# Gate and up from whole-number weights, with the scales applied where PSUM is read, in a quantized FFN on one core

## The chip, the cores and the metric

One NeuronCore of a Trainium2 chip runs the whole program. The metric is the device time of one launch in microseconds, as a median over runs. A profile is one further execution, recorded by the hardware.

## The reference

For x of 2 x 1024 x 512 in float32, `out = x + s * silu(f)`, where s is causal attention with ALiBi over the layer-normed x (32 heads of 16) and f is a gated FFN with int4-like weights on the same normed x. What matters here is the FFN. The weights are whole numbers 0 to 15, with a zero point and a scale for each group of 128 rows and each column:

```python
def dequantize(imatrix, scales, zeros, group_size, out_dtype):
    rs = jnp.repeat(scales, group_size, axis=0)
    rz = jnp.repeat(zeros, group_size, axis=0)
    return ((imatrix.astype(rs.dtype) - rz.astype(rs.dtype)) * rs).astype(out_dtype)
gate = silu(dot(x, gate_proj)); up = dot(x, up_proj)      # 512 -> 1792
f = dot(gate * up, down_proj)                             # 1792 -> 512
```

The group of 128 rows is just one contraction step k of TensorE (512 = 4 x 128). So within one k the scale depends on the output column alone.

## The kernel before

The program is three stages, one after the other: projections and layer norms (0 to about 190 us of the profile), attention in 16 groups of 4 heads (to about 764 us), and the last stage, which is output projection, FFN and combination (764 us to the end).

**Float32 as two parts.** A float32 operand is split into a rounded `fp32r` high part (ACT, a copy) and the rest (a subtraction, DVE or POOL). A product of two such operands takes three matmuls: low x high, high x low, high x high (`terms`).

**In the attention stage** the FFN's weights are made ready beside the attention. A "half job" is 128 x 896 weights: SP loads zeros (broadcast), scales (broadcast) and weights, ACT converts weights and zeros to float (`convert`), POOL subtracts (L799) and multiplies (L802) in the weight buffer `w_f`. There are 24 of them, 16 for gate and up and 8 for down. POOL also forms small vectors for the softmax in between (`chain`), in program order with the jobs.

**In the last stage** the loop `blocks` runs over 4 blocks of 512 tokens (three in a hardware loop, the last by itself). The 4 quarters (u or t) of a block are 128 tokens each. Each block does:
- the attention output of 4 quarters is gathered (ACT `load_o`), transposed (PE L1279, `trans_o`), split (ACT `hi_o`, DVE L1230 `lo_o`) and projected (PE L1301, 12 matmuls for each quarter) into the four single banks `y`; ACT copies the result to `s_sb` (`copy_s`);
- 14 tiles `it` of 128 inner columns. `gate_up` (L1318) is 2 x 4 x 3 = 24 matmuls of 512 columns into a pair of banks, gate in one and up in the other, each an accumulation over all four k. ACT takes Silu of the gate bank (L1188), DVE multiplies by the up bank (L1251) and that is h; ACT copies its high part (`h_hi`), DVE subtracts for the low part (L1253); `down` (L1330) is 12 matmuls into `y`. The weights of each tile are split too: ACT copies three high parts of 128 x 512 (`w_gu`, `w_d`, L1130) and POOL subtracts three low parts (L1089);
- at the end ACT takes Silu of the four `y` banks (L1214), DVE multiplies by `s_sb` (L1262), POOL or DVE adds x (L1124, L1266), SP stores.
- the normed x of the next block is made in between (DVE L1225 `norm`, PE L1288 `trans_x`, ACT `hi_x`, DVE L1236 `lo_x`).

PE's order for a tile is `gate_up(it + 1)` and then `down(it)`, so the chain from the gate bank to the low part of h has a whole `gate_up` to run behind. The eight PSUM banks are four single ones (`y`) and two pairs (`pair`). All orders are written out by hand, each engine runs its own in program order, and semaphores join them.

Of the kernel before, what the change touches and what calls it, by code (L numbers as in the profile page):

```python
# [24 lines left out]
F32 = mybir.dt.float32  # L25
# [7 lines left out]
P = 128  # L33
# [19 lines left out]
ROWS = 111  # L53


def build(nc, x, wproj, lnw, w_all, z_all, s_all, ident_in, identb_in, tri_in, behind_in, qrows, krows, out):
# [7 lines left out]
    with ExitStack() as ctx:  # L64
# [16 lines left out]
        xrstd = sb("xrstd", [P, TILES], F32)  # L81

# [18 lines left out]
        with ExitStack() as ca:  # L101
# [13 lines left out]
            vst = sa("vst", [P, 2, HEADS, VW], F32)  # L115
            st6x = sa("st6x", [P, 6], F32)
# [8 lines left out]
        w_f = sb("w_f", [P, JOBS * INNER], F32)  # L125
# [16 lines left out]
        with ExitStack() as cc:  # L142
            sc = sb_in(cc)
            xc_hi = sc("xc_hi", [P, KT, 512], F32R)
            xc_lo = sc("xc_lo", [P, KT, 512], F32R)

            ws_hi = [sc(f"ws_hi{n}", [P, 3, 512], F32R) for n in range(2)]
            ws_lo = [sc(f"ws_lo{n}", [P, 3, 512], F32R) for n in range(2)]

            h_hi = [sc(f"h_hi{n}", [P, 512], F32R) for n in range(2)]  # L150
            h_lo = [sc(f"h_lo{n}", [P, 512], F32R) for n in range(2)]
            sg = [sg0, sc("sg1", [P, 512], F32)]
            xnc = sc("xnc", [P, 2, D], F32)
# [132 lines left out]
        cst_in, lnw_in, wo_in = sem("cst_in"), sem("lnw_in"), sem("wo_in")  # L286
        wo_hi_done, wo_lo_done = sem("wo_hi_done"), sem("wo_lo_done")
# [33 lines left out]
        with nc.Block() as block:  # L321
            @block.sync
            def _(sp):
                sp.dma_start(xin[:, 0, :], x_t[0]).then_inc(x_in[0], 16)
                for kt in range(KT):
# [6 lines left out]
                  .then_inc(lnw_in, 16)  # L332

# [88 lines left out]
            def _(act):  # L422
# [50 lines left out]
                def body(c, s, q, first, last):  # L473
                    for u in range(2):
                        t = 2 * c + u
                        copy_v(t, u, c)
                        if not (last and u == 1):
                            x_hi(t + 1, 1 - u)
                        if u == 1 and not first:
# [155 lines left out]
            def _(pe):  # L635
# [24 lines left out]
                def qk_trans(t):  # L660
                    for a in range(2):
                        pe.wait_ge(qk_ln, 2 * t + a + 1)
                        if not (isinstance(t, int) and t < 1):
                            pe.wait_ge(part_r, 2 * t - 1 + a)
                        for kt in range(KT):
# [5 lines left out]
                def body(c, s, q, first, last):  # L671
                    for u in range(2):
                        t = 2 * c + u
                        project(t, u, 2, b_v, proj_v, (v_copy, t))
                        if not (last and u == 1):
                            x_trans(t + 1)
                        project(t, u, 0, b_q, proj_q, (qk_clip, 2 * t - 1))
# [33 lines left out]
        z_in, z_conv, z_sub, z_mul = sem("z_in"), sem("z_conv"), sem("z_sub"), sem("z_mul")  # L711

# [21 lines left out]
        with nc.Block() as block:  # L736
            @block.sync
            def _(sp):
                def half_job(jj):

                    if not (isinstance(jj, int) and jj == 0):
                        sp.wait_ge(z_mul, jj)
                    sp.dma_start(zst[:, :].bitcast(I32), z_all[bass.ds(jj, 1), :].to_broadcast([P, HALF])).then_inc(z_in, 16)
                    sp.dma_start(sst[:, :], s_all[bass.ds(jj, 1), :].to_broadcast([P, HALF])).then_inc(z_in, 16)
                    sp.dma_start(w_f[:, bass.ds(jj * HALF, HALF)].bitcast(I32), w_all[bass.ds(jj, 1)].rearrange("a p c -> (a p) c"))\
# [5 lines left out]
                half_job(0)  # L751
# [680 lines left out]
```

## Time and profile before

| | us |
|---|---|
| median of 3 runs | 1297.69 |
| the 3 runs | 1294.58, 1297.69, 1305.38 |
| span of the profiled execution | 1300.7 |
| PE busy in it | 1205.7 (93%) |
| DVE, ACT, POOL busy | 754.4, 626.0, 503.3 |

The busy time of PE counts matmuls that overlap: a matmul of 512 columns is recorded as 0.39 us and the next one starts 0.23 us after it. So the busy share tells that PE has work, not that it runs at its peak. To see the pace one reads starts. "L1330" is a line of the kernel as printed above. "x12" in a merged row is twelve instructions in a row, and a time in square brackets is the idle time before it with the instruction that ended it.

### The profile page before, as it was taken

To read this page: it belongs to the slowest core of one execution; us is meant where nothing else is said; L and a number is where in the kernel's file an instruction comes from. 1 tells how busy PE (TensorE), PEld (TensorE's weight loads), DVE (VectorE), ACT (ScalarE), POOL (GpSimd) and SP (SyncE) were. 2 spreads that over 40 slices of the span, in tenths; PEclk is the share of its full clock that TensorE was granted. 3 is DMA by queue.
4 is the path that set the end of the run, shared out by engine and by line. 5 is a ranking of instruction groups with operands and counts; after the bars stand their busy time and mean duration, and the time that the engine had idled before them with its cause. 6 is when DMAs were issued, how large, how long until landed. Compare 5 with 4: busy or idle time off the path is not lost. (4 is left out here: it accounts for less than half of the span.)

```text
span 1300.7 us, 23572 instructions
## 1 busy us (share of the span) xinstructions
PE 1205.7 (93%) x6848; PEld 768.9 (59%) x6848; DVE 754.4 (58%) x1835; ACT 626.0 (48%) x955; POOL 503.3 (39%) x544
## 2 busy tenths in 40 slices
PE   6999987999999899899998989999999999999997
PEld 5777752333333333333333358887888888888886
DVE  6877887877877778778777622225222522252223
ACT  3333332666666566566665764335433443344332
POOL 2755550313131221212131333555455445545553
PEclk9999986999999999999999989999999999999999
DMA  6234454454546444555565210001100010011000
GB/s 222 91 115 131 138 163 133 116 144 105 147 105 143 99 118 84 125 107 149 107 149 108 83 69 1 1 1 40 57 0 0 32 65 0 0 33 65 1 1 33
DMA packets 101901, 106.62 MB, mean 82 GB/s; under 512 B 28385, under 2 KB 81121, under 8 KB 101729
## 3 DMA queue, kind: packets, MB, share of 16 engines
q1 hardware_dynamic: 75392, 93.10, 27.7%
q10 hardware_dynamic: 26464, 12.98, 3.4%
q8 instruction: 22, 0.36, 0.1%
q14 instruction: 23, 0.18, 0.0%
HBM read 84.41 MB, written 21.23 MB: 81 GB/s over the span
## 5 line engine op out<-in xcount | busy, mean ns | idle before, releaser
L842 ACT ACTIVATE pr<-pair 128x1024 f32<-128x1024 f32 (+3 forms) x384 | 293.6, 811 | 179.7 <-PE pair L965 101.3
L1089 POOL TENSOR_TENSOR ws_lo<-w_f,ws_hi 128x512 fp32r<-128x512 f32 x168 | 238.0, 1445 | 271.8 <-ACT ws_hi L1130 271.8
L264 DVE CUSTOM_DVE_ANT_0 bank<-bank,sg 128x384 f32<-128x384 f32 (+3 forms) x512 | 242.3, 515 | 97.7 <-PE bank L274 94.4
L1251 DVE TENSOR_TENSOR sg<-pair,sg 128x512 f32<-128x512 f32 x56 | 38.8, 692 | 276.0 <-ACT sg L1188 276.0
L1318 PE MATMUL pair<-xc_hi,ws_lo 128*128 128x512 f32 x448 | 175.4, 392 | 0.0
L1318 PE MATMUL pair<-xc_lo,ws_hi 128*128 128x512 f32 x448 | 175.2, 391 | 0.0
L1318 PE MATMUL pair<-xc_hi,ws_hi 128*128 128x512 f32 x448 | 175.1, 391 | 0.0
L267 DVE TENSOR_REDUCE mx<-bank 128x1 f32<-128x512 f32 x256 | 159.8, 683 | 7.4 <-PE bank L274 6.7
L1188 ACT ACTIVATE sg<-pair 128x512 f32<-128x512 f32 x56 | 33.5, 598 | 235.7 <-PE pair L1318 235.6
L799 POOL TENSOR_TENSOR w_f<-w_f,zst 128x896 f32 (+1 forms) x24 | 50.1, 2088 | 215.2 <-ACT zst L856 215.2
L274 PE MATMUL bank<-xin_c,s_sb 108*128 108x512 bf16 (+3 forms) x384 | 118.3, 354 | 13.1 <-DVE mx L264 10.2
L274 PE MATMUL bank<-ks,qs 108*128 108x512 bf16 (+3 forms) x384 | 111.6, 337 | 7.9 <-DVE mx L264 6.9
L1130 ACT ACTIVATE ws_hi<-w_f 128x512 fp32r<-128x512 f32 x168 | 99.1, 627 | 30.2 <-PE bank L1330 28.4
L960 PE MATMUL pair<-qs,ks 111*128 111x512 bf16 (+3 forms) x384 | 97.1, 338 | 16.2 <-DMA qs<-dt 10.4
L960 PE MATMUL pair<-s_sb,xin_c 111*128 111x512 bf16 (+3 forms) x384 | 97.5, 339 | 14.9 <-DMA s_sb<-dt 10.6
L1253 DVE TENSOR_TENSOR h_lo<-sg,h_hi 128x512 fp32r<-128x512 f32 x56 | 71.1, 1271 | 47.7 <-ACT h_hi L1130 47.7
L1318 PEld LDWEIGHTS pair<-xc_hi,ws_hi 128*128 128x128 f32 x448 | 84.6, 189 | 17.7
L1318 PEld LDWEIGHTS pair<-xc_hi,ws_lo 128*128 128x128 f32 x448 | 84.6, 189 | 17.5
L1318 PEld LDWEIGHTS pair<-xc_lo,ws_hi 128*128 128x128 f32 x448 | 84.4, 188 | 17.5
L274 PEld LDWEIGHTS bank<-xin_c,s_sb 108*128 108x128 bf16 x384 | 34.3, 100 | 93.8 <-DVE mx L264 52.2
L1330 PE MATMUL bank<-ws_hi,h_lo 128*128 128x512 f32 x224 | 88.0, 393 | 0.4 <-DVE h_lo L1253 0.2
L1330 PE MATMUL bank<-ws_hi,h_hi 128*128 128x512 f32 x224 | 87.3, 390 | 0.0
(101 smaller groups left out, 1980.0 us busy)
## 6 DMA issues: line engine op xcount, KB each, us to landing
stk<-parts ACTq DMA_DIRECT2D x16, 768.0 KB, 5.9
zst<-in_z_all SPq DMA_DIRECT2D x24, 448.0 KB, 4.2
sst<-in_s_all SPq DMA_DIRECT2D x24, 448.0 KB, 5.0
w_f<-in_w_all SPq DMA_DIRECT2D x24, 448.0 KB, 6.8
xin_c<-in_x SPq DMA_DIRECT2D x32, 256.0 KB, 2.7
s_sb<-stk SPq DMA_DIRECT2D x96, 64.0 KB
xin_c<-stk SPq DMA_DIRECT2D x96, 64.0 KB
qs<-stk SPq DMA_DIRECT2D x96, 64.0 KB
```

What stands on the lines that cost most here:

```text
L264: dve.tensor_tensor_reduce(out=src, in0=src, in1=tri[:, 512 - w:512], scale=1.0, scalar=-3.0e38, op0=ALU.add, op1=ALU.max, accum_out=dst). ...
L267: dve.tensor_reduce(dst, src, AX.X, ALU.max).then_inc(m_free, 1)
L274: pe.matmul(b[:, 0:w], qs[s][0:ROWS_MAX, qt // 4, j, (qt % 4) * P:(qt % 4 + 1) * P], ks[s][0:ROWS_MAX, j, k0:k0 + w], start=True, stop=Tru ...
L799: pool.tensor_tensor(w, w, zst[:, :], ALU.subtract).then_inc(z_sub, 1)
L842: act.activation(pr[e % 3][:, 2 * p:2 * p + 2, 0:w], pair[p][:, :, 0:w], ACT.Exp, scale=SCALE)\
L960: mm = pe.matmul(pair[p][:, jj, 0:512 - c0], ks[s][0:ROWS, j, kt * P:(kt + 1) * P], qs[s][0:ROWS, qb, j, c0:512], start=True, stop=not dia ...
L1089: return pool.tensor_tensor(dst, src, hi.bitcast(F32), ALU.subtract)
L1130: return act.activation(dst, src, ACT.Copy)
L1251: dve.tensor_tensor(sg[s][:, :], pair[s][:, 1, :], sg[s][:, :], ALU.mult).then_inc(h_mul, 1)
L1253: dve.tensor_tensor(h_lo[s][:, :], sg[s][:, :], h_hi[s][:, :].bitcast(F32), ALU.subtract).then_inc(hl_done, 1)
L1318: mm = pe.matmul(pair[s][:, g, :], l, r, start=(k == 0 and n == 0), stop=(k == KT - 1 and n == 2))
L1330: mm = pe.matmul(y[t][:, :], l, r, start=(it == 0 and n == 0), stop=(it == IT - 1 and n == 2))
```

## The change

All of it concerns the FFN.

1. **Weights.** Gate and up weights stay whole numbers after the zero point is taken off (w - z, from -15 to 15). These fit `fp32r` without a rest. So there are no low and high parts of gate and up weights any more: `w_gu` on ACT and POOL is gone, and matmuls read `w_gu`, now the name of the weight buffer itself. In the attention stage POOL's job for these 16 halves is one subtraction (out of a staging buffer) and not two operations; the scale is not loaded in broadcast. The 8 half jobs of down are as before.
2. **Scales.** A small table `sgu` holds the scales with the inner column on the partition: one DMA, one transpose and one ACT copy in the first stage.
3. **Matmuls.** For each tile and each of gate and up, each k has a bank of its own: 8 banks for a tile, 2 matmuls each (w x low part of x, w x high part of x). That is 16 and not 24. The banks are the four of the two pairs (`GB`), used in turn: bank j needs bank j - 4 to be read.
4. **Reading the banks.** ACT reads the k = 0 banks with a scale (`first`, twice for a tile); DVE reads the other six with `scalar_tensor_tensor`: bank * scale + accumulator (`add`). ACT's Silu then works in SBUF, and so does DVE's multiplication (`gate`, two SBUF operands).
5. **Low parts of h and of the down weights** are both made by POOL, in this order for a tile: `h_low(it)`, `w_low(it)`. DVE makes neither.
6. **Order.** PE does all of `gate_up(it)` and then `down(it - 1)` (for tiles 4 to 13). The projection of the attention output is cut in half quarters and lies between the banks of tiles 0 to 2; it uses `y` banks for its transposes, not the pair. ACT's order for a tile is `silu(it - 1)`, `first(it, 0)`, `first(it, 1)`, `h_high(it - 1)`, `w_high(it - 1)`.

The core of the diff:

```diff
-                def w_gu(b, it):
-                    s = it % 2
-                    pool.wait_ge(wg_hi, IT * b + it + 1)
-                    for n in range(2):
-                        mm = low(ws_lo[s][:, n, :].rearrange("p (k c) -> p k c", k=KT), w_cols(n, it),
-                                 ws_hi[s][:, n, :].rearrange("p (k c) -> p k c", k=KT))
-                    mm.then_inc(wg_lo, 1)
...
+                def h_low(b, it):
+                    pool.wait_ge(hh_done, IT * b + it + 1)
+                    pool.tensor_tensor(h_lo[it % 3][:, :], acc[0][it % 2][:, :], h_hi[it % 3][:, :].bitcast(F32), ALU.subtract)\
+                        .then_inc(hl_done, 1)
+
+                def w_low(b, it):
+                    pool.wait_ge(wd_high, IT * b + it + 1)
+                    pool.tensor_tensor(wd_lo[it % 2][:, :], w_down(it), wd_hi[it % 2][:, :].bitcast(F32), ALU.subtract)\
+                        .then_inc(wd_low, 1)
 
                 def body(b, last):
                     for it in range(IT):
...
+                        h_low(b, it)
+                        w_low(b, it)
...
+                def first(b, it, n):
+
+                    act.wait_ge(hl_done, IT * b + it + 1)
+                    act.wait_ge(gu_done, IT * NJ * b + NJ * it + n + 1)
+                    act.activation(acc[n][it % 2][:, :], GB[n], ACT.Copy, scale=scale_of(n, 0, it)).then_inc(ev_first, 1)
+
+                def silu(b, it):
+                    act.wait_ge(ev_add, (NJ - 2) * (IT * b + it) + NJ - 3)
+                    act.activation(acc[0][it % 2][:, :], acc[0][it % 2][:, :], ACT.Silu).then_inc(silu_done, 1)
+
+                def h_high(b, it):
+                    act.wait_ge(h_mul, IT * b + it + 1)
+
+                    act.wait_ge(down_done, C_D + IT * b + it - 2)
+                    copy(h_hi[it % 3][:, :], acc[0][it % 2][:, :]).then_inc(hh_done, 1)
...
+                    for it in range(IT + 1):
+                        if it > 0:
+                            silu(b, it - 1)
+                        if 1 <= it <= 2:
+                            copy_s(b, 2 * it - 2)
+                        if it < IT:
+                            for n in range(2):
+                                first(b, it, n)
+                        if it < 2:
+                            hi_o(b, 2 * it)
+                            load_o(b, 2 * it + 1)
+                        if it == 0:
+                            hi_o(b, 1)
+                            load_o(b, 2)
+                        else:
+                            h_high(b, it - 1)
+                            if it <= 2:
+                                copy_s(b, 2 * it - 1)
+                            if it == 1:
+                                hi_o(b, 3)
+                            w_high(b, it - 1)
...
+                def add(b, it, j):
+
+                    n, k = j % 2, j // 2
+                    dve.wait_ge(gu_done, IT * NJ * b + NJ * it + j + 1)
...
+                    a = acc[n][it % 2][:, :]
+                    dve.scalar_tensor_tensor(out=a, in0=GB[j % 4], scalar=scale_of(n, k, it), in1=a, op0=ALU.mult, op1=ALU.add)\
+                       .then_inc(ev_add, 1)
...
                 def body(b, last):
                     for it in range(IT):
...
+                        if it > 0:
+                            gate(b, it - 1)
+                        for j in range(2, NJ):
+                            add(b, it, j)
+                            if it < 2 and j in (3, 5):
+                                lo_o(b, 2 * it + (j - 3) // 2)
...
+                def gate_up(b, it, pair_of):
+
+                    for j in (2 * pair_of, 2 * pair_of + 1):
+                        n, k = j % 2, j // 2
+                        if j < 4:
+                            if it > 0:
+                                pe.wait_ge(ev_add, (NJ - 2) * (IT * b + it - 1) + j + 3)
+                            elif j == 0:
+                                pe.wait_ge(xc_l, 4 * b + 4)
+                        elif j < 6:
+                            pe.wait_ge(ev_first, 2 * (IT * b + it) + j - 3)
+                        else:
+                            pe.wait_ge(ev_add, (NJ - 2) * (IT * b + it) + j - 5)
+                        w = w_col(n, k, it)
+                        pe.matmul(GB[j % 4], w, xc_lo[:, k, :], start=True, stop=False)
+                        pe.matmul(GB[j % 4], w, xc_hi[:, k, :], start=False, stop=True).then_inc(gu_done, 1)
+
+                def down(b, it, t):
+                    if t == 0:
+                        pe.wait_ge(wd_low, IT * b + it + 1)
+                        pe.wait_ge(hl_done, C_HL + IT * b + it + 1)
...
+                    gate_up(b, 0, 0)
                     trans_o(b, 0)
-                    gate_up(b, 0)
+                    gate_up(b, 0, 1)
                     trans_o(b, 1)
+                    gate_up(b, 0, 2)
+                    s_project(b, 0, 0)
+                    gate_up(b, 0, 3)
+                    s_project(b, 0, 1)
+
+                    gate_up(b, 1, 0)
                     trans_o(b, 2)
+                    s_project(b, 1, 0)
+                    gate_up(b, 1, 1)
+                    s_project(b, 1, 1)
+                    gate_up(b, 1, 2)
                     trans_o(b, 3)
+                    s_project(b, 2, 0)
+                    gate_up(b, 1, 3)
+                    s_project(b, 2, 1)
+
+                    gate_up(b, 2, 0)
+                    s_project(b, 3, 0)
+                    gate_up(b, 2, 1)
+                    s_project(b, 3, 1)
+                    gate_up(b, 2, 2)
+                    down(b, 0, 0)
+                    down(b, 0, 1)
+                    gate_up(b, 2, 3)
+                    down(b, 0, 2)
+                    down(b, 0, 3)
+                    for it in range(3, IT):
+                        for n in range(4):
+                            gate_up(b, it, n)
+                        for back in ((2, 1) if it == 3 else (1,)):
+                            for t in range(4):
+                                down(b, it - back, t)
+                    if not last:
+                        for u in range(4):
+                            trans_x(b + 1, u)
+                    for t in range(4):
+                        down(b, IT - 1, t)
                 blocks(pe, body)
```

Also in the diff: the buffers of the split attention output (`of_hi`, `of_lo`) share memory with `sg`, so `hi_o(b, 1)` waits for the last DVE multiplication (L1262) of the block before; and each block's `trans_o(b, 0)` waits for a Silu of the block before, because it writes a `y` bank.

## Rows read from the trace of the kernel before

**Rows 1.** Windows: busy time (instructions) of PE, PEld, DVE, ACT, POOL, then granted clock, DMA share.
```profile
200.00:760.00 560.00, 506.97 (x3689) 203.77 (x3691) 423.57 (x1337) 350.81 (x477) 134.98 (x208) 0.96 0.50 118
780.00:1300.70 520.70, 509.85 (x2286) 419.43 (x2284) 162.60 (x169) 199.91 (x353) 252.63 (x177) 1.00 0.06 21
```

**Rows 2.** Chain that ended last, in order of time: start us, us, what.
```profile
909.36 0.69 DVE h_lo L1230
910.09 3.03 PE bank L1301 x12
...
996.17 5.44 PE pair L1318 x24
1001.61 2.72 PE bank L1330 x12
1004.33 5.44 PE pair L1318 x24
...
1040.36 0.69 DVE h_lo L1230
```

**Rows 3.** Timeline of one tile: start us, us, engine, line, what, [idle before it].
```profile
1001.22 0.39 PE L1318 MATMUL pair<-xc_hi,ws_hi 128*128 128x512 f32 x1
1001.64 0.60 ACT L1188 ACTIVATE sg<-pair 128x512 f32<-128x512 f32 x1 [4.80 <-PE pair L1318]
1002.27 0.69 DVE L1251 TENSOR_TENSOR sg<-pair,sg 128x512 f32<-128x512 f32 x1 [5.24 <-ACT sg L1188]
...
831.56 4.23 POOL L1089 TENSOR_TENSOR ws_lo<-w_f,ws_hi 128x512 fp32r<-128x512 f32 x3 [3.93 <-ACT ws_hi L1130]
```

**Rows 4.** Timeline: POOL's subtractions with little beside them, and its hand-over to DVE.
```profile
771.67 3.75 POOL L1089 TENSOR_TENSOR ws_lo<-w_f,ws_hi 128x512 fp32r<-128x512 f32 x3 [3.26 <-ACT ws_hi L1130]
1282.90 1.29 POOL L1089 TENSOR_TENSOR ws_lo<-w_f,ws_hi 128x512 fp32r<-128x512 f32 x1 [5.65 <-ACT ws_hi L1130]
106.46 0.92 POOL L383 TENSOR_TENSOR rsq<-vex,mhalf 128x1 f32<-128x1 f32 x1
107.49 0.75 DVE L549 SCALAR_TENSOR_TENSOR qk<-qk,rsq,lnb 128x512 f32<-128x512 f32 x1 [0.46 <-POOL rsq L383]
```

**Rows 5.** Timeline: PE after a wait for the low part of h, until `gate_up` starts.
```profile
926.41 1.37 DVE L1253 TENSOR_TENSOR h_lo<-sg,h_hi 128x512 fp32r<-128x512 f32 x1 [0.86 <-ACT h_hi L1130]
927.83 0.50 PE L1330 MATMUL bank<-ws_hi,h_lo 128*128 128x512 f32 x1
...
930.72 0.39 PE L1318 MATMUL pair<-xc_hi,ws_lo 128*128 128x512 f32 x1
```

**Rows 6.** Single lines over the whole span: times ns min/median/max.
```profile
L542 DVE SCALAR_TENSOR_TENSOR qk<-qk,mvq,lnb x32: 733/752/1573, 26.0 to 184.8; 128x512 f32<-128x512 f32 x32
L1253 DVE TENSOR_TENSOR h_lo<-sg,h_hi x56: 692/1357/1377, 795.5 to 1289.7; 128x512 fp32r<-128x512 f32 x56
L1251 DVE TENSOR_TENSOR sg<-pair,sg x56: 691/692/694, 793.9 to 1288.3; 128x512 f32<-128x512 f32 x56
L1225 DVE TENSOR_SCALAR xnc<-xin_c,xmean,xrstd x16: 542/736/1516, 764.5 to 1160.9; 128x512 f32<-128x512 f32 x16
L264 DVE CUSTOM_DVE_ANT_0 bank<-bank,sg x512: 236/517/737, 184.3 to 742.8; 128x128 f32<-128x128 f32 x43, 128x384 f32<-128x384 f32 x43, 128x512 f32<-128x512 f32 x43, 128x256 f32<-128x256 f32 x42
L799 POOL TENSOR_TENSOR w_f<-w_f,zst x24: 2068/2088/2098, 233.9 to 752.4; 128x896 f32 x21, 128x896 f32<-128x896 f32 x3
```

**Rows 7.** Timeline around the change of block: start us, us, engine, line, what.
```profile
1028.65 1.03 PE L1288 MATMUL pair<-ident,xnc 128*128 128x128 f32 x8
1030.08 1.11 PE L1288 MATMUL pair<-ident,xnc 128*128 128x128 f32 x8 [0.40 <-DVE xnc L1225]
1033.83 1.08 ACT L1214 ACTIVATE sg<-bank 128x512 f32<-128x512 f32 x2
1034.45 5.98 DVE L1262 TENSOR_TENSOR s_sb<-sg,s_sb 128x512 f32<-128x512 f32 x4 [1.58 <-ACT sg L1214]
1037.79 1.28 ACT L1130 ACT_TABLE_LOAD   x1
```

**Rows 8.** Waits in the attention and last stages: engine line waited for: us, times, longest us.
```profile
POOL w_f L799 <- ACT zst L856: 215.2, 24, 10.9
PE pair L960 <- DMA s_sb<-dt: 10.6, 8, 4.0
```

**Rows 9.** Timeline: PE's pace at the lower clock, at the start of the last stage.
```profile
771.97 0.63 PE L1318 MATMUL pair<-xc_lo,ws_hi 128*128 128x512 f32 x1
772.40 0.63 PE L1318 MATMUL pair<-xc_hi,ws_hi 128*128 128x512 f32 x1
```

More of the change, by code:

```diff
@@ L81, in build @@
         xrstd = sb("xrstd", [P, TILES], F32)
+        sgu = sb("sgu", [P, SGU], F32)
         sg0 = sb("sg0", [P, 512], F32)
@@ L478, in body @@
                             x_hi(t + 1, 1 - u)
+                        if first and u == 0:
+                            act.wait_ge(sgu_ps, 1)
+                            act.activation(sgu[:, :], b_t[1][:, 0:SGU], ACT.Copy).then_inc(sgu_done, 1)
                         if u == 1 and not first:
@@ L676, in body @@
                             x_trans(t + 1)
+                        if first and u == 0:
+                            pe.wait_ge(sraw_in, 16)
+                            pe.transpose(b_t[1][:, 0:SGU], sraw[0:SGU, :], ident[0:SGU, 0:SGU]).then_inc(sgu_ps, 1)
                         project(t, u, 0, b_q, proj_q, (qk_clip, 2 * t - 1))
@@ L1042, in build @@
         NB = TOK // 512
-        C_P, C_OTR, C_YS, C_HL, C_ST = 4, 1, 4, 2, 16
+        C_P, C_OTR, C_YS, C_HL, C_ST, C_D, C_YM = 4, 1, 4, 2, 16, 3, 4
+        GB = [pair[n // 2][:, n % 2, :] for n in range(4)]
+        NJ = 2 * KT
         def blocks(eng, body):
@@ L1321, in down @@
-                def down(b, it):
-                    s = it % 2
-                    if it == 0:
-                        pe.wait_ge(s_cp, 4 * b + 4)
-                    pe.wait_ge(wd_lo, IT * b + it + 1)
-                    pe.wait_ge(hl_done, C_HL + IT * b + it + 1)
-                    for t in range(4):
-                        cols = slice(t * P, (t + 1) * P)
-                        for n, (l, r) in enumerate(terms(h_hi[s][:, cols], h_lo[s][:, cols], ws_hi[s][:, 2, :], ws_lo[s][:, 2, :])):
-                            mm = pe.matmul(y[t][:, :], l, r, start=(it == 0 and n == 0), stop=(it == IT - 1 and n == 2))
-                        if it == IT - 1 and t < 3:
-                            mm.then_inc(y_sum, 1)
-                    mm.then_inc(down_done, 1)
+                    if half == 1:
+                        mm.then_inc(s_proj, 1)
@@ new lines, in down @@
+                def down(b, it, t):
+                    if t == 0:
+                        pe.wait_ge(wd_low, IT * b + it + 1)
+                        pe.wait_ge(hl_done, C_HL + IT * b + it + 1)
+                    if it == 0:
+                        pe.wait_ge(s_cp, 4 * b + t + 1)
+                    cols = slice(t * P, (t + 1) * P)
+                    for n, (l, r) in enumerate(terms(h_hi[it % 3][:, cols], h_lo[it % 3][:, cols], wd_hi[it % 2][:, :], wd_lo[it % 2][:, :])):
+                        mm = pe.matmul(y[t][:, :], l, r, start=(it == 0 and n == 0), stop=(it == IT - 1 and n == 2))
+                    if it == IT - 1 and t < 3:
+                        mm.then_inc(y_sum, 1)
+                    if t == 3:
+                        mm.then_inc(down_done, 1)
```

252 lines of the change are left out of this document (103 added, 149 removed).

## The prediction

> **What bounds the kernel now.** I read the windows by stage first. The last stage is 520.7 us at granted clock 1.00, the full one of the two levels, with hardly any DMA [rows 1]. The chain of waits is then almost all PE there: 5.44 us for the 24 matmuls of a `gate_up`, 2.72 us for the 12 of a `down`, with nothing between [rows 2]. So a tile takes 8.16 us and a matmul 8.16/36 = 0.2267 us. DVE and ACT idle about 5 us before each tile's Silu [rows 3]. PE's order gives the chain behind the gate bank a whole `gate_up` to hide in, and it is hidden. One block, from one L1230 row to the same row of the next, is 1040.36 - 909.36 = 131.0 us [rows 2]. The stage is PE bound, so removing matmuls pays until another chain is longer than what is left.
>
> **Matmuls.** A tile goes from 36 to 28 matmuls: 28 x 0.2267 = 6.35 us, 1.81 less, over 56 tiles 102 us. That is the most the change can give. The question is what ends last instead.
>
> **DVE.** Six adds and one product take the place of L1251 and L1253. No row shows `scalar_tensor_tensor` from PSUM. It lies between L1251 (PSUM and SBUF, 0.69 us) and L542 (the same instruction with two SBUF operands and a pointer scalar, 0.75 us) [rows 6]. I take 0.75 us, and 0.65 us from start to start. 6 x 0.65 + 0.7 = 4.6 us, under 6.35. DVE isn't the bound by its sum.
>
> **The wait in each tile.** Now by order, from the start of `gate_up(it)` as zero. A bank's second matmul ends 0.2267(2j + 1) + 0.39 us on, and ACT starts 0.03 us behind a bank [rows 3]. Bank 0 is there at 0.65, bank 1 at 1.10. ACT reads them at 0.65 and 1.15 (two ACT instructions in a row start about 0.5 apart: 1.08 us for two of 0.60 [rows 7]). DVE's adds run from 1.56 to 5.5; banks 4 to 7 are not kept waiting, because bank 6 needs the first add (done 2.3, wanted 2.7) and bank 7 the second (2.95, wanted 3.2). The Silu of this tile is at 4.9, its product at 6.2, so both are far ahead of the next round. But ACT's copy `h_high(it - 1)` stands behind `first(it, 1)` in its queue. It starts at 1.65 and ends at 2.27. POOL then does `h_low(it - 1)` and `w_low(it - 1)` one behind the other, and `down(it - 1)` waits for both. One such subtraction is 1.25 us when little runs beside it (3.75 for three) to 1.29 [rows 4]. I take 2.52 for two: 2.35 to 4.87. POOL to the next engine is 0.1 us (107.38 to 107.49 [rows 4]), so `down` starts at 4.97. PE finished its 16 matmuls at 16 x 0.2267 = 3.63. It stands 1.34 us in every such tile. After a stop the 12 matmuls take 930.72 - 927.83 = 2.89 and not 2.72 [rows 5]. Period: 4.97 + 2.89 = 7.86 us, against 8.16. Tiles 4 to 13 of each block, 10 of 14, run at this period, so most of the 1.81 us is lost to POOL. Bounds: 7.7 with 1.20 for a POOL operation (2.088 x 512/896 from L799, which ran beside the attention's DVE work [rows 6]), 8.2 with 1.41 (4.23/3, beside a DVE instruction with two SBUF operands [rows 3]).
>
> **The rest of a block.** Before, it is 131.0 - 81.6 = 49.4 us. After, from the start of `gate_up(0)`: tiles 0 to 2, one `down` and the projection are 48 + 12 + 48 = 108 matmuls, 24.5 us, and four transposes of 0.45, 26.3. Waits in it. (a) DVE has the four products L1262 of the old block in its queue ahead of the first adds; they took 5.98 us, mixed with POOL's adds [rows 7], and by their start they end 4.5 us into the new block. Then come two adds and `lo_o(0)`, 6.5. The first half projection waits there; PE has 4.9 us of other work and its second transpose waits for ACT, which has a table load of 1.28 first [rows 7]. Together PE stands 1.6. (b) The third transpose writes `y[0]`, so it waits for `copy_s(0)`, which stands in ACT's queue behind `silu(0)`, which waits for the add of bank 6 (9.4) and perhaps a table load: PE stands about 0.6, and restarts cost the like of 0.15 each. Several such short stops add to 3.7. So 30.0 to the end of `down(0)`. Tile 3 has 16 + 24 matmuls, 9.1, and its second `down` finds the POOL work done. At the end four transposes of x (2.0; [rows 7] have 2.3 with a wait of 0.4) hide the chain of tile 13, and `down(13)` is 2.7. Sum 43.8. The first matmul of the next block finds x ready, since `lo_x` ends about 1.3 us before `down(13)`. Bounds for the waits: 1.5 (the products by themselves) to 8 (each hand-over late by a queue place).
>
> **Sum.** Block: 43.8 + 78.6 = 122.4, 8.6 less than 131.0. Three such blocks 25.8. In the last block no transposes hide the chain of tile 13: Silu and product to 6.2, copy to 6.9, POOL to 9.5, `down(13)` to 12.5 after the start of `gate_up(13)`, against 5.44 + 2.72 + about 3 before; that block gains 6.8. In all 32.6.
>
> **Outside the last stage.** POOL loses 16 operations of 2.09 us in attention. L799 waited 215.2 us for ACT's conversions, and PE's own large waits there are for a DMA, 10.6 us [rows 8]. POOL isn't late, so this is nothing; if it were on the path of the softmax vectors it could give at most 16 x 2.09 = 33. One more transpose, copy and small DMA in the first stage cost under 1 us.
>
> 1300.7 - 32.6 = 1268 for the profiled execution. The median lies 3.0 below the span before, so 1265.
>
> **Port or no port.** L1253, with two SBUF operands, is 0.69 alone and 1.36 beside POOL; L1225, with one SBUF operand and pointer scalars, 0.54 and up to 1.52; L264, from PSUM and SBUF, never passes 0.74 though POOL's jobs run beside it [rows 6]. The adds have PSUM, SBUF and a pointer scalar: no row has that. The Trainium skill (SBUF — State Buffer, "Who interferes with whom") says a DVE instruction with at most one SBUF input outside the two-port modes doesn't contend with GpSimd; by that rule, and by L264, the adds are free, and L1225 is slow for its mode and not for its scalars.
>
> **Rivals.**
> - *Adds and POOL exclude each other.* As L1225 has it. POOL's window 2.35 to 4.87 lies over four adds. POOL waits for the running add at each of its two starts, 0.6 us each: period 9.1, 40 x 1.2 = 48 us more, 1313. It decides from a period of 8.7 on. Against it L264. Chance 0.10. By the rule of the Trainium skill's SBUF page it would be 0.
> - *The clock falls.* In the attention stage, where PE is busy 507 of 560 us, the granted clock is 0.96, in the last stage 1.00 [rows 1]; after PE's idle at the start of the stage matmuls start 0.43 apart, the 1.2 GHz level [rows 9]. PE will now stand 1.3 of 7.9 us. A tile at that level takes about 0.8 (the first banks) + 2.3 (`down`) = 3.1 longer; with one tile in six, 7 of 40, 21 us: 1286. The Trainium skill (TensorE: Matmul & The Clock Gate, "A second HAM failure mode: psum-queue depth-cycling") tells of just this, a PE that stops briefly between groups as it cycles through PSUM and loses clock. Against it: stops of 1.3 are far shorter than that at 764. Chance 0.08.
> - *Startup of blocks stalls at every hand-over*, 4 x 4.3 more: 1282. Chance 0.08.
> - *No wait in the tiles*, if the 7.86 were wrong and PE stayed the bound: 40 x 1.5 less, 1205. The order in the diff speaks against it. Chance 0.04.
>
> **How the numbers follow.** 0.70 for the forecast, with its own range 1251 to 1282: period 7.7 to 8.2 is -6 to +14 us, the waits at the start of blocks -9 to +17, not all at once. About 1% is what a measurement of this kernel can tell from no change, so 1285 is the border. Range for 8 in 10: 1249 to 1290, which leaves out the first and the last rival. Faster: 0.66 of the forecast, 0.04, and 0.05 of the clock and startup rivals, 0.75. Slower: the port rival and a little more, 0.11. Same 0.14.
>
> **What would show it.** In the profile after: period of tiles 4 to 13 (7.9); PE idle before `down` about 1.3 us, released by POOL `h_lo` or `wd_lo`; POOL subtractions of 1.25 to 1.3; adds of 0.70 to 0.75 also while POOL runs; granted clock 1.00; blocks of 122 us; first `down` 30 us after the first `gate_up`. Wrong if POOL operations are 1.7 or more, if the adds stretch, if PE's stop comes before `gate_up` (then DVE is the bound), or if attention's time moves.

## The result

The changed kernel takes 1240.04 us (median of 4 runs, 1237.77 to 1240.87) against 1301.37 before (4 runs): a ratio of 0.9521, 95% interval 0.9474 to 0.9568. It is 61 us faster; the forecast said 33 and its range ended at 1249. In a second series it was 1239.01 against 1297.53, ratio 0.9535 (0.9466 to 0.9605).

The profiled execution has a span of 1236.0 us, 64.7 less than the one of before. I cut both at the same places: the first DMA of the attention stage (`behind`) and the first `norm` of the last stage. Windows of the kernel before; the columns are those of [rows 1]:

```profile
0.00:205.90 205.90, 177.96 (x800) 135.41 (x801) 166.69 (x329) 65.28 (x109) 109.28 (x154) 0.93 0.45 141
205.90:764.50 558.60, 505.34 (x3712) 204.18 (x3712) 418.69 (x1328) 352.59 (x481) 134.98 (x208) 0.97 0.50 118
764.50:1300.70 536.20, 522.37 (x2336) 429.33 (x2336) 169.02 (x178) 208.14 (x366) 259.06 (x182) 0.99 0.07 22
```

The same of the kernel after:

```profile
0.00:197.20 197.20, 175.60 (x801) 134.45 (x802) 166.95 (x329) 65.56 (x110) 109.27 (x154) 0.94 0.47 148
197.20:731.10 533.90, 494.57 (x3712) 201.07 (x3712) 416.81 (x1328) 350.28 (x480) 101.45 (x192) 0.99 0.40 110
731.10:1236.00 504.90, 433.90 (x1888) 337.49 (x1888) 313.29 (x458) 215.80 (x366) 163.87 (x126) 0.99 0.07 23
```

The last stage gives 31.3 us. The forecast for it was 32.6. But the attention stage gives 24.7 and the first stage 8.7, where the forecast had nothing. PE has the same 3712 matmul records in the attention stage of both, but they keep it busy for 505.3 us before and 494.6 after: part of the gain there is the granted clock.

Now the last stage after, the chain of waits in order of time. The last four rows are the same pattern one tile on:

```profile
898.78 0.67 ACT up L1191
900.55 0.74 issue
901.29 1.28 POOL wd_lo L1140
902.69 3.03 PE bank L1375 x12
906.81 0.67 ACT sg L1191
908.59 0.74 issue
909.33 1.29 POOL wd_lo L1140
910.73 3.01 PE bank L1375 x12
```

One tile lasts 910.73 - 902.69 = 8.04 us. Before it was 8.16 [rows 2]. PE's 12 matmuls of `down` start 0.12 us behind the end of POOL's `wd_lo`. The timeline of the same stretch shows what lies ahead of that:

```profile
905.55 0.39 PE L1364 MATMUL pair<-xc_lo,w_gu 128*128 128x512 f32 x1
906.21 0.69 ACT L1191 ACTIVATE gate<-pair,sgu 128x512 f32<-128x512 f32 x1 [2.98 <-PE pair L1365]
906.79 0.68 ACT L1191 ACTIVATE sg<-pair,sgu 128x512 f32<-128x512 f32 x1
907.36 0.63 ACT L1160 ACTIVATE h_hi<-gate 128x512 fp32r<-128x512 f32 x1
908.07 1.31 POOL L1135 TENSOR_TENSOR h_lo<-gate,h_hi 128x512 fp32r<-128x512 f32 x1 [5.51 <-ACT h_hi L1160]
909.01 0.39 PE L1365 MATMUL pair<-xc_hi,w_gu 128*128 128x512 f32 x1
909.33 1.28 POOL L1140 TENSOR_TENSOR wd_lo<-w_d,wd_hi 128x512 fp32r<-128x512 f32 x1
910.63 0.63 ACT L1195 ACTIVATE gate<-gate 128x512 f32<-128x512 f32 x1 [2.12 <-DVE gate L1281]
910.73 0.49 PE L1375 MATMUL bank<-wd_hi,h_lo 128*128 128x512 f32 x1 [1.33 <-POOL wd_lo L1140]
```

The reader should see two things. PE has sent its last `gate_up` matmul at 909.01 and stands 1.33 us until POOL is through. And ACT's copy of `h_hi` (907.36) could have started earlier: DVE had finished its product at 904.05, and the copy only stands behind the two bank reads in ACT's queue. The waits of PE in this stage (us in total, times, longest us) say the same in sum:

```profile
PE bank L1375 <- POOL wd_lo L1140: 55.2, 44, 1.5
PE bank L1323 <- ACT oin_v L1160: 5.3, 4, 2.1
```

And the adds, which no row of before had (times in ns: shortest, median, longest). In most tiles POOL runs beside four or five of the six. This row is half of the 336 adds; the other half lies between 735 and 746 ns:

```profile
L1281 DVE SCALAR_TENSOR_TENSOR gate<-pair,sgu,gate x168: 735/743/753, 737.9 to 1220.3; 128x512 f32<-128x512 f32 x168
```

### The profile page after: what moved, and what is told of

Read it like the earlier page. It is cut to its first block and busy times, and to the rows that moved or that the text cites. A ratio compares the mean times of both kernels' runs of the same rounds, so it can differ in the third digit from the quotient of the medians.

```text
span 1236.0 us, 23869 instructions
## 1 busy us (share of the span) xinstructions
PE 1104.1 (89%) x6401; PEld 673.0 (54%) x6401; DVE 897.0 (73%) x2115; ACT 631.6 (51%) x956; POOL 374.6 (30%) x472
## 5 line engine op out<-in xcount | busy, mean ns | idle before, releaser
L1281 DVE SCALAR_TENSOR_TENSOR gate<-pair,sgu,gate 128x512 f32<-128x512 f32 x168 | 125.3, 746 | 170.3 <-PE pair L1365 170.2
L1364 PE MATMUL pair<-xc_lo,w_gu 128*128 128x512 f32 x448 | 177.7, 397 | 1.8 <-DVE xc_lo L1264 1.8
L1365 PE MATMUL pair<-xc_hi,w_gu 128*128 128x512 f32 x448 | 175.1, 391 | 0.0
L1375 PE MATMUL bank<-wd_hi,h_lo 128*128 128x512 f32 x224 | 91.9, 410 | 55.2 <-POOL wd_lo L1140 55.2
L283 PE MATMUL bank<-xin_c,s_sb 108*128 108x512 bf16 (+3 forms) x384 | 116.7, 349 | 13.2 <-DVE mx L273 10.2
L1364 PEld LDWEIGHTS pair<-xc_lo,w_gu 128*128 128x128 f32 x448 | 84.4, 188 | 26.2 <-DVE sg L1281 3.8
L1365 PEld LDWEIGHTS pair<-xc_hi,w_gu 128*128 128x128 f32 x448 | 84.3, 188 | 15.9
L1375 PE MATMUL bank<-wd_lo,h_hi 128*128 128x512 f32 x224 | 87.7, 391 | 0.0
L1375 PE MATMUL bank<-wd_hi,h_hi 128*128 128x512 f32 x224 | 87.6, 391 | 0.0
L670 PE MATMUL bank<-wq_hi,xt_lo 128*128 128x512 f32 x192 | 79.3, 413 | 5.1 <-DVE xt_lo L533 5.1
L1011 PE MATMUL bank<-pr,oin_v 128*17 128x512 f32 (+3 forms) x768 | 80.6, 491 | 0.0
```

The lines of the kernel that those rows point to most:

```text
L283: pe.matmul(b[:, 0:w], qs[s][0:ROWS_MAX, qt // 4, j, (qt % 4) * P:(qt % 4 + 1) * P], ks[s][0:ROWS_MAX, j, k0:k0 + w], start=True, stop=Tru ...
L670: mm = pe.matmul(b[:, :], l[:, u, kt, :], r[:, kt, cols], start=(kt == 0 and i == 0), stop=(kt == KT - 1 and i == 2))
L1011: mm = pe.matmul(b_o[32 * j:32 * j + VW, c0:512], vs[s][:, kt, j * VW:(j + 1) * VW], pr[e % 3][:, j, 0:512 - c0], start=(kt == 0), stop=(k ...
L1281: dve.scalar_tensor_tensor(out=a, in0=GB[j % 4], scalar=scale_of(n, k, it), in1=a, op0=ALU.mult, op1=ALU.add)\
L1364: pe.matmul(GB[j % 4], w, xc_lo[:, k, :], start=True, stop=False)
L1365: pe.matmul(GB[j % 4], w, xc_hi[:, k, :], start=False, stop=True).then_inc(gu_done, 1)
```

## The experiments

Two questions were open: does POOL's pair set the tile, as the forecast had it, and where do the 33 us outside the last stage come from. This table gives all runs. The runs were made in series, and each ratio is to the runs of the kernel before in the same series; their medians were 1299.11 us (a0 to a3), 1297.53 (b1, b2, c1, d0), 1294.71 (b3, e1, e2) and 1296.51 (f1). "Less than before" below means less than these. Stage lengths are from each kernel's profiled execution, cut as above. They are one execution each, and that of the kernel before was a long one (1300.7 us), so a difference of stages can come out some us larger than that of the medians.

| kernel | median, us | ratio to before (95%) | first stage | attention | last stage |
|---|---|---|---|---|---|
| before | 1301.37 | 1 | 205.9 | 558.6 | 536.2 |
| after | 1240.04 | 0.952 (0.947-0.957) | 197.2 | 534.0 | 504.8 |
| a0_order | 1301.48 | 1.002 (0.998-1.006) | 202.4 | 560.8 | 537.0 |
| a1_no_scale_load | 1280.74 | 0.987 (0.982-0.992) | 203.5 | 541.9 | 536.5 |
| a2_no_scale_mul | 1292.48 | 0.994 (0.991-0.998) | 205.6 | 555.3 | 536.7 |
| a3_neither | 1281.05 | 0.989 (0.983-0.994) | 205.3 | 535.8 | 536.2 |
| d0_after_again | 1239.01 | 0.954 (0.947-0.961) | 197.7 | 533.6 | 506.2 |
| c1_scale_load_back | 1247.29 | 0.958 (0.951-0.965) | 196.8 | 545.3 | 504.5 |
| b1_weights_early | 1193.47 | 0.919 (0.912-0.926) | 197.3 | 534.5 | 458.0 |
| b2_h_high_first | 1192.22 | 0.917 (0.910-0.923) | 197.3 | 533.7 | 459.8 |
| b3_h_high_first_from_4 | 1179.22 | 0.911 (0.907-0.915) | 197.6 | 534.7 | 448.8 |
| e1_pad_before | 1279.53 | 0.988 (0.984-0.993) | 198.4 | 539.6 | 536.7 |
| e2_pad_after | 1249.16 | 0.965 (0.961-0.969) | 203.3 | 536.0 | 504.9 |
| f1_neither_and_pad | 1271.45 | 0.981 (0.978-0.984) | 198.3 | 536.1 | 537.2 |

### The attention stage: order, loads or POOL

**a0_order.** The kernel before with only the order of the half jobs changed. This is the part for SP; POOL and ACT are numbered to match:

```diff
-                def half_job(jj):
+                def half_job(ip, n):
 
-                    if not (isinstance(jj, int) and jj == 0):
-                        sp.wait_ge(z_mul, jj)
+                    jj = half_of(ip, n)
+                    if not (isinstance(ip, int) and 3 * ip + n == 0):
+                        sp.wait_ge(z_mul, 3 * ip + n)
```

> The kernel before with the half jobs of the attention stage in the order of the changed kernel (two of gate and up, then one of down, in each pair of groups), nothing else. Theory 'traffic or POOL': the order alone does nothing, attention stage 555 to 562 us, time within 0.3% of before. Theory 'order': the order of the loads is what made the attention stage of the changed kernel 25 us shorter, then this kernel takes about 1275.

1301.48 us, no change. The order is not it.

**a1_no_scale_load.** As a0, and the kernel leaves out the scale load of gate and up (ACT's waits for the loads count one less):

```diff
-                    sp.dma_start(sst[:, :], s_all[bass.ds(jj, 1), :].to_broadcast([P, HALF])).then_inc(z_in, 16)
+                    if n == 2:
+                        sp.dma_start(sst[:, :], s_all[bass.ds(jj, 1), :].to_broadcast([P, HALF])).then_inc(z_in, 16)
...
-                    pool.tensor_tensor(w, w, sst[:, :], ALU.mult).then_inc(z_mul, 1)
+                    pool.tensor_tensor(w, w, (sst if n == 2 else zst)[:, :], ALU.mult).then_inc(z_mul, 1)
```

> As a0, and the broadcast load of the scales is left out for the 16 halves of gate and up; POOL still does its second operation for them, with the zeros as operand, so these weights are scaled wrongly. Theory 'traffic': 16 loads of 448 KB delay the small transfers that PE waits for (dt to qs) and the clock falls behind the waits; without them the attention stage is 15 to 25 us shorter, 1275 to 1283. Theory 'POOL': POOL's second operation is what delays; then no change here, 1297 to 1301.

1280.74 us, 18 less than before. It is in the attention stage: 541.9, against 558.6 before and 560.8 in a0.

**a2_no_scale_mul.** As a0, and the kernel leaves out POOL's multiplication for gate and up:

```diff
+                    if n < 2:
+                        pool.tensor_tensor(w, w, zst[:, :], ALU.subtract).then_inc(z_mul, 1)
+                        return
                     pool.tensor_tensor(w, w, zst[:, :], ALU.subtract).then_inc(z_sub, 1)
```

> As a0, and POOL's multiplication by the scales is left out for the 16 halves of gate and up (their scales are not applied anywhere); the scales are still loaded. Theory 'traffic': no change, 1297 to 1301. Theory 'POOL': attention stage 15 to 25 us shorter, 1275 to 1283. If the moment of the next loads counts (they start 2.1 us sooner), something between.

1292.48 us, 7 less than before, where a1 has 18; the interval of the ratio (0.991 to 0.998) allows 3 to 12. So POOL's multiplication is not the main cause. What it does give may be POOL's time or the sooner start of the next loads, and the run can't tell.

**a3_neither.** Both edits.

> As a0, without the scale load and without POOL's multiplication for the 16 halves of gate and up: the attention stage of the changed kernel beside the last stage of the kernel before. Both theories: 1270 to 1280, attention stage about 534 us, last stage 536 us. If it is 1297 or more, the 25 us of the attention stage come from neither but from the spread between executions or from the first stage.

1281.05 us, the same as a1: once the scale load is gone, leaving out POOL's multiplication too gives nothing that the medians show. The attention stage is 535.8, near the 534.0 of the kernel after, and the first stage stayed at 205.3. So taking the load away is enough for most of the gain in the attention stage, and something else made the first stage shorter.

What the loads do can be read in the waits of the attention stage (us in total, times, longest us). PE waits there for a transfer of 12 KB, from `dt` to the row of the scores' left operand. In the kernel before:

```profile
PE pair L960 <- DMA s_sb<-dt: 10.6, 8, 4.0
PE pair L960 <- DMA qs<-dt: 10.4, 6, 4.5
```

The first row stands among [rows 8]; the second I had seen and left out. In a0, a1, a2 and a3 in turn:

```profile
PE pair L966 <- DMA s_sb<-dt: 11.0, 7, 4.4
PE pair L966 <- DMA qs<-dt: 7.8, 7, 2.9
```

```profile
PE pair L967 <- DMA s_sb<-dt: 5.9, 4, 5.2
PE pair L967 <- DMA qs<-dt: 1.5, 2, 1.0
```

```profile
PE pair L969 <- DMA s_sb<-dt: 14.5, 8, 4.9
PE pair L969 <- DMA qs<-dt: 0.2, 1, 0.2
```

```profile
PE pair L970 <- DMA s_sb<-dt: 5.1, 2, 4.5
```

And the kernel after:

```profile
PE pair L996 <- DMA s_sb<-dt: 4.0, 1, 4.0
```

From before to after, 21.0 us in 14 waits became 4.0 in one, and that one is the first of the stage. The clean comparison is a0 with a1, where only the load differs: 18.8 us became 7.4. A half job had three transfers of 448 KB in a0, and in a1 those of gate and up have two. The wait for 12 KB is thus for the most part a price of the other traffic; that the transfers meet in the same DMA engines is my reading of it, not something that a run shows by itself. The granted clock follows: 0.96 in this stage in a0 and 0.98 in a1, and PE's busy time for the same 3712 records falls from 510.3 to 500.5 us. By this reckoning the 18.9 us by which the stage is shorter are about half wait (11.4) and half clock (9.8; the two add up to a little more than the whole).

**c1_scale_load_back.** The other way round: the changed kernel with the load put back, into a place that is overwritten unread. (It is not the place of the kernel before.)

```diff
-        Z_IN = (32, 64, 112)
+        Z_IN = (48, 96, 144)
...
+                    if n < 2:
+                        sp.dma_start(w_d[:, bass.ds(ip * HALF, HALF)], s_all[bass.ds(jj, 1), :].to_broadcast([P, HALF])).then_inc(z_in, 16)
                     if n == 2:
```

> The changed kernel with the broadcast load of the gate and up scales put back in the attention stage, into a place that nothing reads before it is overwritten. Theory 'traffic': the attention stage takes back 15 to 25 us, 1255 to 1265. Theory 'POOL' or 'order': 1240, no change.

1247.29 us: 8 more than d0_after_again (below) of the same series, where 15 to 25 were expected. The attention stage took 545.3 and not 533.6, and the wait is back (4.8 of it is the first of the stage, which d0 has too with 3.8):

```profile
PE pair L998 <- DMA s_sb<-dt: 10.8, 6, 4.8
```

The direction is as the theory has it, the size half. Here the load costs 8 us, in the kernel before it cost 18 to 21 (a1 against before and against a0). Something else in the kernel before made it dearer; the next section has a candidate.

### The first stage: addresses

Up to here the first stage was 202.4 to 205.9 us in the kernel before and the four made from it, and it is 196.8 to 197.7 in the changed kernel and the four made from it without a new buffer (d0 repeats it). Run to run it does not change sides. In the first stage the change adds a small load, a transpose and a copy, and one buffer, the table `sgu` of 448 bytes a partition, ahead of nearly all others.

**e1_pad_before.** The kernel before and nothing but this:

```diff
         xrstd = sb("xrstd", [P, TILES], F32)
+        pad = sb("pad", [P, 112], F32)
```

> The kernel before with an unused buffer of 448 bytes a partition where the changed kernel has its table of scales, so that the buffers behind it get the addresses of the changed kernel. Theory 'addresses': the first stage goes from 202 to 206 us to 197, as in all kernels made from the changed one, time 6 to 9 us less, about 1291; the loads in it land sooner (raw_qkv 7.3 us before, 6.7 after). Theory 'the new table's transpose and copy shift the first stage's phases': no change, first stage 202 to 206, 1299.

1279.53 us, ratio 0.988 (0.984 to 0.993): an unused buffer makes the kernel 15 us faster. The first stage is 198.4 as expected, and the attention stage 539.6 and not 558.6, which was not. The waits for the 12 KB transfer shrink to a third though all the loads are there:

```profile
PE pair L961 <- DMA s_sb<-dt: 4.5, 4, 3.6
PE pair L961 <- DMA qs<-dt: 2.4, 4, 1.2
```

**e2_pad_after.** The changed kernel with 64 bytes more, so that the shift is 512 in all:

```diff
         sgu = sb("sgu", [P, SGU], F32)
+        pad = sb("pad", [P, 16], F32)
```

> The changed kernel with 64 unused bytes a partition behind the table of scales, 512 with it, so that the buffers behind get the alignment of the kernel before. Theory 'addresses': first stage 202 to 206 and not 197, time 6 to 9 us more, about 1247. Theory 'phases': no change, 1239.

1249.16 us, 10 more than the kernel after in its second series (15 by the ratios), first stage 203.3. Both directions agree: it is where the buffers lie. The attention stage stays short, 536.0: there the shift hardly costs anything once the scale load is gone. By the sizes in the listing, `s_sb`, `xin_c` and the buffers behind them start 64 bytes past a multiple of 128 in the kernel before and in e2, and on a multiple of 128 in the kernel after and in e1 (`s_sb` at 19,520 and 19,968 bytes from the first buffer). Some transfers land sooner. In the lists of DMA issues (KB each, median us from issue to landing), before and e1:

```profile
stk<-parts ACTq DMA_DIRECT2D x16, 768.0 KB, 5.9
xin<-in_x SPq DMA_DIRECT2D x16, 256.0 KB, 3.1
```

```profile
stk<-parts ACTq DMA_DIRECT2D x16, 768.0 KB, 5.3
xin<-in_x SPq DMA_DIRECT2D x16, 256.0 KB, 2.8
```

The kernel after has 5.0 and 2.9 there, e2 5.7 and 3.1. DVE waited 15.4 us for `xin` in the first stage before, 10.2 in e1, 9.1 after, 14.7 in e2. The three transfers of a half job do not follow: 4.2, 5.0 and 6.8 us before, 4.3, 5.1 and 6.7 in e1. So why PE's waits in the attention stage shrink in e1 is not shown. Which boundary it is (128 bytes, 256 or 512) was not tried. The Trainium skill (DMA: Bandwidth & Descriptors, "How a descriptor splits into AXI transactions") says that the first transaction of a descriptor which doesn't start on a multiple of 256 bytes starts at the boundary below, and that the unused bytes before the start still cost time on the bus. The runs agree that the start matters; they don't show that this is how.

**f1_neither_and_pad.** Both causes at once in the kernel before (the edits of a3 and e1). Like a3 it leaves out the scales of gate and up.

> The kernel before with both causes found outside the FFN at once: the unused 448 bytes (e1), and no scale load and no POOL multiplication for the gate and up halves (a3; those scales are applied nowhere). Its last stage is that of the kernel before. Theory 'the two overlap in the attention stage, because either one takes away the late transfers': first stage 198, attention 533 to 536, last 536.5, 1268 to 1272, so that the changed kernel lies below it by the last stage alone, 31 us. Rival 'they add': attention about 517, 1254.

1271.45 us; first stage 198.3, attention 536.1, last 537.2. The two causes overlap in the attention stage: 19 us by addresses (e1), 23 by loads and POOL (a3), 22.5 by both. The medians have 15, 18 and 25 in all. So at the shifted addresses load and multiplication together are worth only 8 to 10 us in the kernel before as well (f1 against e1, from series to series), as the load is in the changed kernel (c1): the addresses are the likely reason why it cost 18 to 21 in a1. From here to the kernel after only the last stage is left: 537.2 against 504.8 in the profiles, 31 us in the medians of separate series.

### The tile: what ends last

**d0_after_again** is the changed kernel as the measure for its series.

> The changed kernel once more, as the measure for the others on the same chip. 1240. Its first stage tells whether the 8.7 us by which that stage was shorter (197.2 against 205.9) belong to the change or differ from one execution to the next: 195 to 206 are both possible.

1239.01 us, first stage 197.7.

**b1_weights_early.** The split of the down weights one tile ahead, so that `down` waits for one POOL operation:

```diff
                 def body(b, last):
+                    w_low(b, 0)
                     for it in range(IT):
                         h_low(b, it)
-                        w_low(b, it)
+                        if it + 1 < IT:
+                            w_low(b, it + 1)
...
                             load_o(b, 2)
+                            w_high(b, 0)
...
-                            w_high(b, it - 1)
+                            if it < IT:
+                                w_high(b, it)
```

> The changed kernel with the split of the down weights one tile ahead: ACT's w_high and POOL's w_low of tile it stand where those of tile it - 1 stood, so down(it - 1) waits for one POOL operation and not for two. Theory 'POOL pair sets the tile' (my prediction): tiles 4 to 13 go from 8.03 to 6.8 us, 40 x 1.23 = 49 us, 1191. Theory 'DVE sets the tile': no change, 1240. Theory 'PE sets it, the wait is hidden': no change.

1193.47 us, 46 less than the kernel after, where 49 were expected. POOL's `h_lo` rows give the new tile, 949.57 - 942.83 = 6.74 us:

```profile
942.83 1.30 POOL L1135 TENSOR_TENSOR h_lo<-gate,h_hi 128x512 fp32r<-128x512 f32 x1 [4.18 <-ACT h_hi L1162]
944.09 1.29 POOL L1140 TENSOR_TENSOR wd_lo<-w_d,wd_hi 128x512 fp32r<-128x512 f32 x1
949.57 1.31 POOL L1135 TENSOR_TENSOR h_lo<-gate,h_hi 128x512 fp32r<-128x512 f32 x1 [4.19 <-ACT h_hi L1162]
```

The pair of POOL operations did set the tile, and DVE did not. PE waited 55.2 us for POOL in the last stage after, and 4.2 here.

**b2_h_high_first.** As b1, and ACT's copy ahead of the two bank reads from tile 3 on:

```diff
                             silu(b, it - 1)
+                            if it > 2:
+                                h_high(b, it - 1)
...
-                            h_high(b, it - 1)
                             if it <= 2:
+                                h_high(b, it - 1)
                                 copy_s(b, 2 * it - 1)
```

> As b1, and from tile 3 on ACT makes the high part of h before it reads the first two banks of the next tile, so POOL's h_low starts 1.6 us sooner. Theory 'the chain through ACT's queue sets what is left': tiles 4 to 13 reach PE's own 6.35 us, 18 us less than b1, 1173. Rival: DVE, with about 4.6 us of work in each tile behind a later start, becomes the bound; then b2 is like b1 or slower, 1190 or more.

1192.22 us, the same as b1: the expected 1173 did not come. Yet the tile is shorter, 945.18 - 938.76 = 6.42 us:

```profile
938.76 1.29 POOL L1135 TENSOR_TENSOR h_lo<-gate,h_hi 128x512 fp32r<-128x512 f32 x1 [3.68 <-ACT h_hi L1162]
945.18 1.30 POOL L1135 TENSOR_TENSOR h_lo<-gate,h_hi 128x512 fp32r<-128x512 f32 x1 [3.45 <-ACT h_hi L1162]
```

PE's waits show a new one, once in each block:

```profile
PE pair L1370 <- ACT gate L1193: 8.3, 4, 2.1
```

It is in tile 3. ACT has `w_high(2)` in its queue, which waits for `down(0)` to end, and then the Silu, the product and the copy, all before it reads the first bank that PE wants to refill. Behind this stop, eight matmuls start 0.43 us apart, the lower of the clock's two levels (compare [rows 9]):

```profile
883.53 0.50 PE L1370 MATMUL pair<-xc_lo,w_gu 128*128 128x512 f32 x1 [2.06 <-ACT gate L1193]
885.02 0.63 PE L1370 MATMUL pair<-xc_lo,w_gu 128*128 128x512 f32 x1
885.45 0.63 PE L1371 MATMUL pair<-xc_hi,w_gu 128*128 128x512 f32 x1
```

The granted clock of its last stage is 0.97, against 0.99 in b1. Such a stretch of 6 to 8 matmuls costs about 1.5 us (7 x 0.2). I count six in the last stage of b2, three of them behind the four stops in tile 3, and one in b1. So the stops (8.3 us) and the clock (some 7) together eat what the shorter tile gives, 40 x 0.32 = 13 us.

**b3_h_high_first_from_4.** The same with the early copy from tile 4 on (`it > 3`).

> As b2, but the early high part only from tile 4 on: in b2 PE waited 2.1 us in tile 3 of each block and the granted clock fell behind it. Theory 'the chain through ACT's queue sets what is left, and b2 lost it again in tile 3 and to the clock': 4 x 2.1 and some 8 us for the clock less than b2, 1175 to 1183. Rival 'DVE or the clock takes the gain anyway': 1190.

1179.22 us (1177.1 to 1182.9), as expected. The wait for ACT is gone, 8.3 of the 11.0 us by which the last stage is shorter than in b2; four stretches at the lower clock are left, and the clock of the stage is 0.98. This is the fastest kernel here, 0.911 of before (0.907 to 0.915).

## Why the prediction was wrong

**The last stage was right in its mechanism, and its total in part by luck.** The forecast had 32.6 us; the profiles show 31.3 and 30.0 (d0). Its steps one by one:

- *Period of tiles 4 to 13*: 7.86 forecast, 8.04 measured, from three small terms. ACT's copy with a scale takes 0.69 us and not 0.60, and puts two starts 0.57 and 0.58 apart where I had 0.5; POOL's pair took 2.54 (908.07 to 910.61) and I had 2.52; PE's restart was 0.12 behind it.
- *DVE*: adds of 0.75 us, 0.65 apart, as taken. *Ports*: all 336 adds take 0.735 to 0.753 us although POOL runs beside most of them. That rival is out. The rule of the Trainium skill (SBUF — State Buffer, "Who interferes with whom"), that a DVE instruction with at most one SBUF input outside the two-port modes doesn't contend with GpSimd, holds here with a pointer scalar beside that input.
- *Blocks*: two starts of `of_lo` a block apart are 987.5 - 862.4 = 125.1 and 1110.9 - 987.5 = 123.4, against 122.4 forecast and 131.0 before. By the first `gate_up` matmul of each block, the four blocks gain 9.5, 6.0, 7.5 and 5.7 us, 28.7 in all, where the forecast had 8.6 for three and 6.8 for the last. The other 2.6 us come from the stretch between the first `norm` of the stage and its first `gate_up` matmul, 7.1 us before and 4.5 after, for which the forecast had no term: blocks forecast 4 us too well and this stretch left out nearly cancel.
- *Start of a block*: `down(0)` ended 27.9 to 30.9 us behind the first `gate_up`, forecast 30.0. The four products L1306 took 4.77 us and not the 5.98 taken from [rows 7], and ended 3.6 us into the new block where I had 4.5. PE's stop for ACT's `load_o` was 2.1 us, where all the first stops together were put at 1.6.
- *Clock*: granted 0.99 in the last stage after, with PE stopping 1.3 us in each of 40 tiles and no matmul at the lower clock there. That rival is out for these stops. At the start of a block it did happen once in the kernel after, behind a stop of 2.1 us:

```profile
862.17 0.66 PE L1323 MATMUL bank<-ident,oin_v 128*128 128x128 f32 x4 [2.07 <-ACT oin_v L1160]
864.11 0.63 PE L1346 MATMUL bank<-wo_lo,of_hi 128*128 128x512 f32 x1
864.53 0.63 PE L1346 MATMUL bank<-wo_hi,of_hi 128*128 128x512 f32 x1
```

  Seven matmuls ran at that pace. The like stop of the next block (987.23, 2.07 us) was followed by none, nor were the two of d0. In b2 and b3 it happened more often.
- *No wait in the tiles* is out: PE waited 55.2 us for POOL.

**The step that failed is "Outside the last stage".** It held that POOL's shorter jobs are worth nothing, since PE's own waits there are for a DMA, and that the rest of the first stage costs under 1 us. POOL's price was a little low: a2 gives 0.6% (0.2 to 0.9), 7 us, at most. What failed is that the step priced POOL's instructions and not the loads that the change takes away, although it named, one sentence on, PE's waits for a DMA. I used them as proof that POOL isn't late, and never asked what those DMAs wait for. The change removes 16 broadcasts of 448 KB; a1 shows 18 us for that, about half of it shorter waits and half a higher clock behind them. Also, I quoted one row of two ([rows 8]: 10.6), so the wait looked half its size.

**The second part of the miss no view of before could price.** A new buffer of 448 bytes moves nearly all others, and by e1 and e2 that alone is worth 10 to 15 us. It is also why the first stage became shorter although it has more to do: the term of under 1 us for the table was not wrong, the shift beside it was missing. The full diff (not the part printed above) does put it ahead of the others, and the rule that the start of a descriptor matters was in the Trainium skill (DMA: Bandwidth & Descriptors, "How a descriptor splits into AXI transactions"); I did not look at addresses. But neither sign nor size could be worked out from rows.

The two are not additive in the attention stage (f1). In sum: 31 us from the last stage, and 25 to 30 from loads, POOL and addresses together (f1 lies 25 below before in its own series, ratio 0.981, interval 0.978 to 0.984). The range ended at 1249 since each rival that I priced lay in the last stage; a term "transfers that PE waits for go away", 21 us by the rows of before, would have put the forecast at 1244 and the result well inside its range.

Still open: which boundary the addresses have to meet and by what mechanism, why the load is worth 18 us at one set of addresses and 8 at the other, what gave the 7 us of a2 (POOL's time, or the moment of the next loads), and why one stop of 2.1 us costs PE its clock and the next one doesn't.

## What to carry to other kernels

When a change takes a transfer away, price it by the waits for *other* transfers that run at the same time, small ones above all, and by the clock that these waits cost, and not by the wait for its own. Before two versions are compared, look whether buffers moved: an unused buffer is a cheap test, and was worth 1.2% here. And where an engine waits for two operations of another, ask for each whether it had to be done in this round: `w_low` did not, and moving it one tile ahead gave more (46 us) than the whole change had given in that stage.

## What the runs showed of the hardware

- Moving the buffers by 448 bytes a partition took a kernel of 1295 us to 1280 (e1, 1.2%), with the same instructions. A shift of 512 in place of 448 made the changed kernel 10 us slower (e2, 1249.16 against 1239.01).
- A 12 KB transfer cost PE 18.8 us of waiting in 14 waits with three transfers of 448 KB in each half job (a0), and 7.4 in 6 with two in those of gate and up (a1). With three and the shifted addresses it was 6.9 in 8 (e1).
- `scalar_tensor_tensor` from PSUM with a pointer scalar takes 0.74 us for 128 x 512 float32, whether or not POOL runs. The product of two SBUF operands takes 0.69 us alone; where it met POOL's subtraction in b2 it took 1.27 (880.97).
- ACT's copy from PSUM with a scale from SBUF takes 0.69 us, 0.09 more than the plain one (`copy_s`, 0.60).
- PE kept its full clock with a stop of 1.3 us in each 8 us. Behind stops of 2.1 us it fell to the lower level in some places (after at 862.17, b2 at 883.53) and not in others (after at 987.23, b2 at 1107.04).
